# The payload's bias as one product for 26 columns, and the count of a key row moved ahead of the near rows' head

## The reference

```
x = x + layer0(relu(layernorm(x)), edge_index, ...)   # softmax over edges of the same src
x = x + layer1(relu(layernorm(x)), edge_index, edge_attr_64, ...)
# in layer1, for every edge and each of 8 heads:
scores = sum(q[dst] * k[src]) * scale + (edge_features @ We + be)
e = exp(scores - segment_max(scores, dst)); denom = segment_sum(e, dst)
agg = segment_sum(e / denom[dst] * v[src], dst)
x = x + layer2(...);  x = x + layer3(...)
```

## Time and profile before

| | |
|---|---|
| median of three runs | 12159.75 us |
| profiled execution | 12157.44 us, span 12155.7 us |
| PE busy | 1455.4 us (12%) |
| DVE busy | 7516.9 us (62%) |
| ACT busy | 5311.8 us (44%) |
| POOL busy | 8285.0 us (68%) |
| TensorE's granted clock | 0.515 of full speed |

### The profile page before, as it was taken

How to read it: one execution, slowest core, us unless ns; L and a number is a source line. 1 busy time by engine, 2 the same in 40 slices (tenths; PEclk the granted TensorE clock), 3 DMA queues, 4 the chain that set the end, 5 groups by cost and what they waited for, 6 DMA issues and landing times.

```text
span 12155.7 us, 59249 instructions
## 1 busy us (share of the span) xinstructions
PE 1455.4 (12%) x5450; PEld 1244.1 (10%) x5450; DVE 7516.9 (62%) x7339; ACT 5311.8 (44%) x5435; POOL 8285.0 (68%) x8734
## 2 busy tenths in 40 slices
PE   2104544445100000021000000200000000000001
PEld 1103444444100000010000000200000000000001
DVE  8734555555288888857999999544444553333333
ACT  1034444444166666634666666333333333333332
POOL 1037777777577777756777777577777767777776
PEclk7555555555555555555555555555555555555555
DMA  4735666666366666635666666233333333333333
GB/s 167 268 101 184 203 205 206 204 202 206 91 213 211 215 214 211 213 119 179 214 214 214 214 214 214 75 111 110 113 112 110 112 90 100 106 106 106 103 106 103
DMA packets 795658, 1963.17 MB, mean 162 GB/s; under 512 B 214907, under 2 KB 423251, under 8 KB 794914
## 3 DMA queue, kind: packets, MB, share of 16 engines
q1 hardware_dynamic: 461770, 1140.56, 26.5%
q0 software_dynamic: 333856, 822.30, 23.9%
HBM read 1220.42 MB, written 741.78 MB: 161 GB/s over the span
## 4 chain that ended last, share of the span: by engine, by line
DVE 27%; POOL 24%; issue 21%; DMA 10%; ACT 8%; PE 7%; SPq 1%; DVEq 1%; ACTq 0%; POOLq 0%
POOL region L1158 22%; DVE work L1306 8%; DMA region<-start_rows_by_src 5%; DVE psB L1214 4%; PE psR L1073 3%; PE psR L1074 3%; ACT work L1389 3%; DMA region<-x,ix_s 2%; DVE work L1242 2%; DVE psR L1246 2%; DVE region L563 2%; DVE psR L1299 2%; DVE region L564 2%; ACT psB L1337 2%; POOL work L1559 1%
## 5 line engine op out<-in xcount | busy, mean ns | idle before, releaser
L1306 DVE TENSOR_TENSOR_SCAN work<-work,psR 128x1792 f32<-128x1792 f32 (+2 forms) x496 | 1971.5, 3975 | 91.7 <-DVE ix_s L1229 56.0
L1324 ACT COPY work<-region 128x1664 f32<-128x1664 f32 (+1 forms) x496 | 1166.6, 2352 | 1892.4 <-DMA region<-start_rows_by_dst 964.4
L1214 DVE TENSOR_TENSOR_SCAN psB<-psB,work 128x1792 f32<-128x1792 f32 (+1 forms) x496 | 1485.2, 2994 | 695.3 <-ACT psB L1337 629.5
L1158 POOL DMA_INDIRECT region<-kv,ix_s x1612 | 1524.1, 945 | 568.2 <-issue 455.2
L1158 POOL DMA_INDIRECT region<-qm,ix_s x1612 | 1524.5, 946 | 526.2 <-issue 454.9
L1158 POOL DMA_INDIRECT region<-x,ix_s x1612 | 1521.1, 944 | 528.8 <-issue 458.6
L1158 POOL DMA_INDIRECT region<-k,ix_s x1612 | 1521.4, 944 | 521.0 <-issue 514.0
L1158 POOL DMA_INDIRECT region<-h,ix_s x1612 | 1521.2, 944 | 491.4 <-issue 490.8
L1389 ACT COPY work<-work 128x1664 f32<-128x1664 f32 (+3 forms) x620 | 1573.8, 2538 | 0.0
L1388 ACT COPY psR<-work 128x128 f32<-128x128 f32 (+2 forms) x496 | 190.3, 384 | 2627.5 <-DVEq L1307 2627.5
L1242 DVE TENSOR_TENSOR work<-region,psB 128x1664 f32<-128x1664 f32 x372 | 702.4, 1888 | 563.9 <-DMA work<-keyrow,row_i 382.0
(11 more groups left out here) (296 smaller groups left out, 5909.6 us busy)
## 6 DMA issues: line engine op xcount, KB each, us to landing
region<-start_rows_by_dst SPq DMA_DIRECT2D x248, 832.0 KB
state_p<-work SPq DMA_DIRECT2D x124, 936.0 KB
state_p<-work SPq DMA_DIRECT2D x124, 884.0 KB
start_rows_by_src<-zero_t SPq DMA_DIRECT2D x1, 103168.0 KB, 275.4
region<-start_rows_by_src SPq DMA_DIRECT2D x124, 832.0 KB
start_rows_by_dst<-zero_t SPq DMA_DIRECT2D x62, 1664.0 KB, 8.0
state_pA<-work SPq DMA_DIRECT2D x124, 832.0 KB
state_p<-work SPq DMA_DIRECT2D x124, 832.0 KB
```

The costliest lines, as they stand in the source:

```text
L1158: g_.indirect_dma_start(rows_s[b][:, k, 0:wd_s], None, q.tabs, bass.IndirectOffsetOnAxis(ap=ix_s[b][:, k:k + 1], axis=0))\
L1214: nc.vector.tensor_tensor_scan(near_ps[:, 0:m], near_ps[:, 0:m], zt[:, 0:m], 0.0, ALU.mult, ALU.add).then_inc(q.s("held"), 1)
L1306: c.do(nc.vector.tensor_tensor_scan(st[:, 0:F * (K + 1)], decay_at(q, b)[:, 0:F * (K + 1)], summed[:, 0:F * (K + 1)], 0.0, ALU.mult, ALU.add))
L1324: nc.scalar.copy(f_by_t(zt, q.HF)[:, :, 1:K + 1].rearrange("p f t -> p t f"), rows_d[b][:, :, :].rearrange("p t w -> p (t w)")[:, 0:K * q. ...
```

## The change

Two edits, both in the first pass, and the load that the first one needs.

```
-        be2 = sb("be2", [1, 16])
+        be2 = sb("be2", [1, KE, 8])
...
-                load(be2[:, j * 8:(j + 1) * 8], row("L1_gnn_be"))
+                load(be2[:, j * K:(j + 1) * K, :], row("L1_gnn_be").unsqueeze(1).to_broadcast([1, K, 8]))
...
+                nc.tensor.matmul(sum_ps[:, PAY_AT:PAY_AT + PAY_N], ones[0:1, :], be2[:, :, :].rearrange("p t w -> p (t w)"), start=True, stop=False)
                 for u in range(KE // 2):
-                    at = sum_ps[:, PAY_AT + u * 16:PAY_AT + (u + 1) * 16]
-                    nc.tensor.matmul(at, attrT[:, u, :], we2[:, :], start=True, stop=False)
-                    ins = nc.tensor.matmul(at, ones[0:1, :], be2[:, :], start=False, stop=True)
+                    ins = nc.tensor.matmul(sum_ps[:, PAY_AT + u * 16:PAY_AT + (u + 1) * 16], attrT[:, u, :], we2[:, :], start=False, stop=u == KE // 2 - 1)
...
+                    if q is PB and b:
+                        count_act(1, i, row1)
                     if q is PB and not final:
                         near_start_act(act, q, i + b, 1 - b)
                     if q.near is not None and not last:
                         near_rows_act(act, q, i + 1, b)
                     if q is PB:
                         (payload_made_act if b else payload_turned_act)(act, i)
-                        if b:
-                            count_act(1, i, row1)
-                            act.wait_ge(S("nt_counted"), i + (NB + 1))
+                    if q is PB and b:
+                        act.wait_ge(S("nt_counted"), i + (NB + 1))
```

## The result

The changed kernel takes 12123.25 us, the median of 7 runs (12119.17 to 12126.3). The kernel before, in 7 runs beside it, has a median of 12159.75 (12159.2 to 12212.4). The ratio of the two is 0.9962, 95% interval [0.9949, 0.9975]: faster, by less than half a per cent. The median lies 2.75 us under the forecast of 12126. The two differ because one run of before took 12168.47 and one 12212.4, which pulls its mean and not its median: the means of before and after are 12168.4 and 12123.3, a ratio of 0.9963.

The account below looks back on a forecast made before the run. The near load's loop (34.42 us) was taken to bound the first pass through holes in GpSimd's gathers. Holes 29.3 plus pass end 4.3 gave 33.6 off 12157.4: 12123.8, plus 2.3, so 12126 us; forecast's own range 12118 to 12134, overall 12116 to 12157.

Parts of the forecast that it names:

- The reading of the bound: First pass: near load's loop of 34.42 us exceeds GpSimd's 33.72 a turn, costing 29.3 us through 14 holes between gathers.
- Step (1): TensorE's product block in each first-pass turn: ends 6.2 us earlier, so the 2.29 us wait before the payload copy goes.
- Step (3): First-pass loop falls to 32.13 us, under GpSimd's 33.72; near load stops slipping, all 14 holes close: -29.3 us.
- Step (4): End of the first pass, last key row to load for the next spread: -2.4 and -1.9, together -4.3 us.
- the last line of the sum: Final conversion: profiled 12157.4 - 33.6 = 12123.8, plus 2.3 for the median of the runs, so 12126 us.
- The guess about a space that comes round by the number of transfers: Every fourth first-pass turn GpSimd reaches transfer-list space that must be free of the last key row, making a hole.
- The rule weighed, VectorE's port: GpSimd can't write descriptors while VectorE holds the shared port; holes would stay, only the end's 4.3 us gained: 12155.
- Step (2), the moved count: Count of 1.77 us moved ahead of the near rows' head on ScalarE: zero, bounds -1.8 to +1.8 a turn.
- The rival that I gave for "slower", a near load that lands later: First-pass near load takes 13 us to land in place of 10.1, loop 35.0 us: 12210 us; 3 in 100.
- the 112 us priced in that step for VectorE's product: Cost if the moved count's 1.8 us delay to VectorE's next product isn't covered: 62 x 1.8 = 112 us.

Follow-up runs that it names:

- b_shift: Kernel before plus ten gathers ahead of the first pass into a buffer nobody reads: 12202.38 us, ratio 1.0025 to the kernel before.
- the product alone: Kernel before with only the wide bias product, count left behind the payload copy: 12124.84 and 12121.58 us quick; 13812.22 us slow, ratio 0.9988.
- again_b: Changed kernel with both edits, rerun against the kernel before on the third occasion, a slow one: 13986.74 us, ratio 1.0123.
- the count alone: Kernel before with only the count moved ahead of the near rows' head, 26 products kept: 12121.92 us quick; 14280.68 us slow, ratio 1.0315.

## Why the prediction was right, and where it was wrong

Right, by its own steps, on the condition it was made for:

- The reading of the bound. The near load's loop, not a wait that the profile names, cost 29.3 us in the 14 holes (added up, their idle time beyond 0.30 us is 29.8). With the loop at 33.7 us all of them close; the pass is 30.1 us shorter between key rows, and three different kernels that shorten the loop end at the same time.
- Step (1): the wait of 2.29 us goes and the copy of the near rows is what is late next. A term of it was mis-sized: TensorE's block is 6.7 us, not 7.9. The wide product takes 1.06 us in place of 0.8, but the 13 others take 0.44 each in place of 0.54, now that no one-row product stands between them. It changes nothing, as that step had said of any price up to 2.1.
- Step (3): forecast 8.3 us from near load to key row and a landing after 4.3; measured 9.2 and 3.9 in the turn shown.
- Step (4): forecast 4.3, measured 4.5. The pass starts 1.9 us later (982.1 for 980.2), already so before it begins; no step had that. Together 1.9 - 30.1 - 4.5 = -32.7; the span lost 32.8.

Wrong:

- The step that failed is the last line of the sum: "The median of the runs is 2.3 above it, so 12126." It holds for medians, 12159.75 and 12123.25. But it takes the kernel before as one number, from three runs. Of 55 runs 15 were 20 to 80 us longer, and none of 61 with either edit. The sum puts at nothing, without a reason, what the change takes off the long runs: 8.7 us in the mean of before (12168.4 - 12159.75), which turns 0.9970 by medians into 0.9963 by means. So the mechanism was right, and a term beside it was missing. That either edit removes the scatter is shown. Why isn't: it may be that two loops of 33.7 and 34.4 us push each other, but no profile fell on a long run, so where it loses its time stays open. That `b_shift`, with longer holes, has its median at 12202 speaks for more and longer holes, and proves nothing.
- The guess about a space that comes round by the number of transfers: `b_shift` speaks against it, with the reserve given there. It carried no term. What the holes wait for is open. The table of transfer queues for 940 to 3200 us of the kernel before, with its 14 holes, has in it:

```profile
q14 instruction: 2, 0.02, 0.0%
q8 instruction: 1, 0.02, 0.0%
```

  Queue, kind, packets, MB, share. The Trainium skill, Runtime: NRT & Kernel Launch, "Instruction fetch mechanics", says that a taken branch whose target is outside the two pages in reach makes the engine fetch by a transfer and stall. By that rule the holes would be loads of the loop's code. The profile shows three packets of that kind for 62 turns and 14 holes, and the same three in the changed kernel, which has no hole. So as far as it records them the holes are not such loads.
- The rule weighed, VectorE's port. That "the same instruction beside the sixth gather makes no hole at 1088.86" is misread: that product starts at 1085.70 and is over at 1087.59, before the gather. The changed kernel shows what the sentence wanted: the product of 2604.03 to 2605.92 lies over the starts and ends of gathers that keep their 0.30 us. The section of the Trainium skill that the prediction names (SBUF — State Buffer, "SBUF: two separate sides") also ties the lock to a VectorE instruction in a two-port mode, or to one with two inputs in SBUF; this product has one input in SBUF and one in PSUM, TensorE's output memory (`psB`), and no run shows its mode.
- Step (2), the moved count: "On this path it moves nothing: zero". True on the quick condition, where GpSimd never waited for the count. The step weighed what is queued behind the count on ScalarE; it did not weigh who waits for the count itself. That is GpSimd, at `nt_counted`, and on the slow occasions this wait is 10 us a turn and, by the reading above, holds back gathers that would hold back TensorE. There the moved count costs 3.15%. The rival that I gave for "slower", a near load that lands later, is not what happened; nor is the 112 us priced in that step for VectorE's product.
- So the chance of 3 in 100 for slower holds for the quick condition alone: with both edits the kernel was 1.2% slower on one of the four occasions on which it ran, the only slow one.

The version to keep is the product alone: 0.9959 and 0.9963 where the kernel before takes 12160, and 0.9988 [0.9974, 1.0003] where it takes 13830. It wasn't run beside both edits on a slow occasion.

## What to carry to other kernels

Where no engine waits by name and a stream still has holes, look for a second loop that is a little slower than the stream. Here the gain is the difference of the two and not the work taken out, and once the loop is under the stream's pace nothing more comes. When an instruction is moved earlier, ask who waits for it and what that waiter will then start sooner: a wait that reads as nothing in a quick run can be the one that paces the kernel in a slow one. And take the spread of the kernel before as a part of its time: with a few runs, the median of before can leave out what the change removes.

## What the runs showed of the hardware that was not expected

- The same kernel took 12160 us on two occasions and 13820 to 13930 on three. In the first pass (1000 to 3000 us) the transfers ran at 204 and 159 GB/s, which is no more than the same bytes over a longer turn (204 x 34.2 / 43.55 = 160). No engine works more slowly: a gather is busy 0.94 us and the product of 128x1664 on VectorE 1.89 us in both. What differs is how long engines stand still, in good part for reasons that the profile can't name.
- In the slow condition TensorE (2.65 us between products, or a last product of which ScalarE hears 20 us late) is held up while GpSimd issues gathers, and most often let go 3 to 7 us after the last one starts; in `again_b` half of such waits, the shorter half, end between gathers. The transfers aren't at their limit then: from 2489 to 2507 us of the count alone they run at 70 GB/s, with the 16 DMA engines busy for a quarter of the time. What holds TensorE is open.
- 13 products of 16 columns with 128 rows take 0.44 us each back to back, and 0.54 where each alternates with one of a single row. One of 208 columns with a single row takes 1.06. The granted clock was 0.51 to 0.52, TensorE's lower level of 1.2 GHz.
